# Sums over queries placed directly ahead of the next tile's sums over keys, from the tenth step on

## The chip, the cores and the metric

One Trainium2 chip, one of its cores. The metric is device time in microseconds (us), the median of several runs. Engines are TensorE (PE, its weight loads PEld), VectorE (DVE), ScalarE (ACT), GpSimd (POOL) and SyncE (SP), which only issues transfers here. Each engine runs its own list of instructions in order; semaphores order them against each other. PSUM has eight banks of 128 x 512 floats, and matmuls write there alone.

## The reference, cut to what matters

A macaron block over 4096 tokens of width 256: half a mixture of experts, an attention layer with its own hidden layer, and again half a mixture of experts. The change lies in the attention layer, whose softmax-free form sums over the 16 heads of one token:

```
q, k, v = (xn @ wq + bq), (xn @ wk + bk), (xn @ wv + bv)      # each b n (16 heads) (16 dims)
fq = elu(q) + 1 ; fk = elu(k) + 1
kv    = einsum('bhnd,bhne->bnde', fk, v)                      # sums over keys, per token
qkv   = einsum('bhnd,bnde->bhne', fq, kv)                     # sums over queries, per token
qk    = einsum('bhnd,bnd->bhn', fq, fk.sum(axis=1))
x     = q_x + (qkv / (qk + 1e-6)) @ wo + bo
h     = gelu(ln(x) @ fc_w + fc_b, approximate=False)
out   = x + h @ proj_w + proj_b
```

The mixture of experts routes each token to one of eight experts with a capacity, and passes the others on unchanged.

## The kernel before

The kernel has three phases: the first experts, a middle loop, and the second experts. The middle loop (lines 595, 803, 1044, 1622 and 2085, one for each engine) takes the 32 tiles of 128 tokens through the attention layer in a software pipeline of 43 steps, counted from 0. In step s, tile s-2 gets q, k and v (`qkv`), tile s-4 its sums over keys (`sum_kv`) and tile s-5 its output (`turn_o`, `project`); tile s-6 enters the hidden layer. Every group of four tiles then goes through the hidden layer (`up_mid`, `down_mid`), two of eight hidden slices a step, from step 10 on. From step 14 on finished groups are also routed for the second experts: turned, given logits, chosen (`choose`), counted, dispatched.

All orders are written out by hand. On PE a step before the change goes: turn of zn (tile s-2); `up_mid` (even slice); in every fourth step logits; `sum_kv(s-4)`; `turn_o(s-5)`; `qkv(s-2)`; `down_mid` (odd slice of the step before); `turn_kv(s-4)`; in two of four steps a turned tile; `project(s-5)`; turn of hn (tile s-6); `up_mid` (odd slice); `sum_att(s-4)`; a turned tile or a count; `down_mid` (even slice).

A tile's attention is this chain. `sum_kv` writes bank B_ATT by 32 products of 128 x 32 weights (`keys`, `values`). ACT copies it to `kvt` (`copy_kvt`), PE turns it into bank B_KV, DVE copies it to `kv` (line 1679). `sum_att` multiplies `kv` with `queries`, again 32 products of 128 x 32 weights, into B_ATT. DVE's `attended` transposes that to `att`, adds and inverts the denominator (`den`) and writes `on`. `turn_o` turns `on` into B_KV; ACT copies that as `ots` (high part, line 1063), DVE writes the low part (`low_o`, line 1569), and `project` multiplies both with `o_w` into bank B_V. DVE adds it to z as `xo` (line 1685) and takes statistics of it; POOL makes the root, and DVE hn. In steps 14, 18, 22, ... DVE's `add_rest` (line 1613, four additions) stands behind these statistics. It empties the down banks into `x_`, and the first `down_mid` of the next group, at the end of the same step, waits for it (`s_x2`).

On ACT a step goes: copy of zn's turn, two gelus of the even slice, `copy_kvt`, the copy of o, the exp table, relu, exp and the copy of v (`qkv`), the copy of hn's turn, two gelus of the odd slice. On DVE: low part of zn, z, `low_o`, zn, statistics and routing steps, x1, the features (line 1673), `kv`, `xo` with its statistics, `add_rest`, low part of h, statistics of the next x1, hn, and from step 10 on `attended` last of all. On POOL: the subtraction of hidden parts (line 795) of the even slice, roots and `xr`, the subtraction of the odd slice.

Three variables in PE's loop (`turn_free`, `v_free`, `kv_free`) hold the semaphore after which a shared bank may be written again.

## Time and profile before

| | us |
|---|---|
| runs (three) | 727.66, 728.11, 729.62 |
| median | 728.11 |
| span of the profiled execution | 726.3 |
| PE busy | 670.9 |
| DVE busy | 481.1 |
| ACT busy | 420.1 |
| POOL busy | 326.5 |

The span runs from the first to the last instruction; some 1.8 us of the median lie around it. TensorE's granted clock is 1.00 of its upper level (2.4 GHz) in every stretch of rows 2 below. Busy times overlap, and a busy PE only says that a product was in flight: the places where PE waits are seen by the idle times in front of an instruction, given in brackets with what ended them. Of the loop, steps 10 to 33 take from 232.5 to 528.8 us, steps 34 to 42 the 68 us behind.

### The profile page before, as it was taken

The page shows a single profiled execution, that of the slowest core. Times are in us where ns is not written, and L with a number is a line of the kernel's source. Part 1 is how long each engine was busy: PE and PEld are TensorE (multiplying, and loading weights), DVE is VectorE, ACT ScalarE, POOL GpSimd, SP SyncE. Part 2 cuts the span into 40 slices and gives each one's busy share as a digit, 9 for nine tenths or more (in the row PEclk, how much of TensorE's full clock was granted, in tenths as well). Part 3 has the DMA queues.
Part 4 walks back from the last instruction along what each step waited for, and adds up shares of the span by engine and source line. Part 5 has one row for each costly group of instructions (what it writes and reads, how often), then busy time and mean ns, then how long its engine had stood idle before and what let it go on. Part 6 is the DMA issues. An engine that isn't in the chain of part 4 may idle for free.

```text
span 726.3 us, 17454 instructions
## 1 busy us (share of the span) xinstructions
PE 670.9 (92%) x6214; PEld 567.6 (78%) x6214; DVE 481.1 (66%) x1332; ACT 420.1 (58%) x841; POOL 326.5 (45%) x493
## 2 busy tenths in 40 slices
PE   7689999998777999999999999999999885999994
PEld 5449999975566788888888888888888663999994
DVE  7856757425688766767777768677676565777751
ACT  5755556502334767676767676766754642766660
POOL 5234563122232453545573664745547563353312
PEclk9879999999999999999999999999999998999998
DMA  8479788404656444544555555555433343567720
GB/s 264 149 241 322 229 270 276 139 29 119 98 99 109 91 66 90 95 87 66 101 86 85 117 84 129 68 108 91 86 73 96 116 132 109 167 215 217 219 93 29
DMA packets 287104, 95.56 MB, mean 132 GB/s; under 512 B 213989, under 2 KB 284737, under 8 KB 287019
## 3 DMA queue, kind: packets, MB, share of 16 engines
q1 hardware_dynamic: 272298, 85.48, 48.9%
q0 software_dynamic: 3840, 8.32, 3.6%
q10 hardware_dynamic: 10880, 0.66, 1.0%
q8 instruction: 50, 0.82, 0.5%
q14 instruction: 36, 0.29, 0.1%
HBM read 65.09 MB, written 29.40 MB: 130 GB/s over the span
## 4 chain that ended last, share of the span: by engine, by line
PE 75%; DVE 8%; issue 6%; ACT 4%; POOL 2%; DMA 2%; SPq 1%; ACTq 1%; POOLq 0%; DVEq 0%
PE bank L1735 68%; PE bank L1744 7%; DMA qkv_rows<-feats 1%; POOL hids L795 1%; SPq L373 1%; ACTq L373 1%; ACT hids L1038 1%; DMA x_all<-in_L_attn_q_x_dram 1%; ACT feats L1001 1%; POOL table L677 1%; ACT feats L999 0%; DVE kv_ L1679 0%; ACT ots L1063 0%; DVE sth L1687 0%; DVE att_ L1576 0%
## 5 line engine op out<-in xcount | busy, mean ns | idle before, releaser
L1735 PE MATMUL bank<-down_w,hids 128*128 128x256 f32 x768 | 105.8, 286 | 1.9 <-POOL hids L795 1.6
L1735 PE MATMUL bank<-hnts,up_w 128*128 128x512 f32 x384 | 104.4, 407 | 0.0
L795 POOL TENSOR_TENSOR hids<-hid,hids 128x512 fp32r<-128x512 f32 x64 | 83.1, 1298 | 41.0 <-ACT hids L1038 40.6
L1735 PEld LDWEIGHTS bank<-down_w,hids 128*128 128x128 f32 x768 | 95.7, 188 | 6.2 <-POOL hids L795 3.4
L1735 PE MATMUL bank<-qkv_w,xnts 128*128 128x256 f32 (+1 forms) x384 | 76.4, 346 | 5.7 <-DVE xnts L1589 4.8
L1735 PEld LDWEIGHTS bank<-hnts,up_w 128*128 128x128 f32 x384 | 67.5, 189 | 11.4
L1735 PEld LDWEIGHTS bank<-qkv_w,xnts 128*128 128x128 f32 x384 | 60.6, 189 | 18.2 <-DVE xnts L1589 7.5
L1035 ACT ACTIVATE hid<-bank,cols 128x512 f32<-128x512 f32 x64 | 44.1, 688 | 45.8 <-PE bank L1735 45.5
L786 POOL TENSOR_SCALAR sth<-sth 128x1 f32<-128x1 f32 x32 | 7.2, 226 | 125.3 <-DVE sth L1601 125.3
L1735 PE MATMUL bank<-a_w,xa_h 128*128 128x256 f32 x256 | 60.2, 379 | 0.0
L1735 PE MATMUL bank<-xa_xt,a_w 128*128 128x256 f32 x384 | 55.1, 294 | 1.4 <-DVE xa_xt L1327 1.4
L1735 PE MATMUL bank<-xb_xt,b_w 128*128 128x256 f32 x384 | 52.9, 287 | 1.4 <-DVE xb_xt L1327 1.4
L1735 PEld LDWEIGHTS bank<-xa_xt,a_w 128*128 128x128 f32 x384 | 49.0, 189 | 3.1 <-DVE xa_xt L1327 1.6
L900 ACT ACTIVATE xa_h<-bank,cols 128x256 f32<-128x256 f32 x64 | 26.8, 470 | 40.8 <-PE bank L1735 40.8
L1735 PEld LDWEIGHTS bank<-a_w,xa_h 128*128 128x128 f32 x256 | 46.3, 190 | 5.1
L1735 PEld LDWEIGHTS bank<-xb_xt,b_w 128*128 128x128 f32 x384 | 48.5, 188 | 2.4 <-DVE xb_xt L1327 1.6
L900 ACT ACTIVATE xb_h<-bank,cols 128x256 f32<-128x256 f32 x64 | 26.9, 471 | 35.0 <-PE bank L1735 35.0
L1569 DVE TENSOR_TENSOR ots<-bank,ots 128x256 fp32r<-128x256 f32 x32 | 13.5, 423 | 50.4 <-ACT ots L1063 50.4
L984 ACT CAST xnts<-bank 128x256 fp32r<-128x256 f32 x32 | 12.0, 374 | 59.9 <-PE bank L1744 57.5
L1038 ACT ACTIVATE hids<-bank,cols 128x512 fp32r<-128x512 f32 x64 | 43.6, 681 | 0.0
L1290 DVE TENSOR_TENSOR b_w<-b_raw,b_w 128x512 fp32r<-128x512 f32 x32 | 23.9, 748 | 22.4 <-ACT b_w L876 22.1
L711 POOL DMA_INDIRECT out_dram<-xb_fin,xb_slot x16 | 17.1, 1067 | 48.2 <-DVE xb_fin L1350 46.1
(272 smaller groups left out, 1546.9 us busy)
## 6 DMA issues: line engine op xcount, KB each, us to landing
qkv_rows<-feats SPq DMA_DIRECT2D x32, 384.0 KB, 3.4
a_raw<-in_L_ffn_w_dram SPq DMA_DIRECT2D x32, 256.0 KB, 4.1
a_w<-in_L_ffn_w_dram SPq DMA_DIRECT2D x32, 256.0 KB, 3.7
b_raw<-in_L_ffn_w_dram SPq DMA_DIRECT2D x32, 256.0 KB, 3.2
b_w<-in_L_ffn_w_dram SPq DMA_DIRECT2D x32, 256.0 KB, 3.0
mid_rows<-x_all SPq DMA_DIRECT2D x8, 512.0 KB, 2.9
x<-mid_rows SPq DMA_DIRECT2D x32, 128.0 KB, 2.4
values<-qkv_rows SPq DMA_DIRECT2D x32, 128.0 KB, 2.9
```

Of the source, the lines that this page charges most:

```text
L373: engine.dma_start(keys[i][t * HEADS:(t + 1) * HEADS, :, t * HD:(t + 1) * HD], qkv_rows[1, rows, :].rearrange("(s t) (h d) -> t h s d", t= ...
L677: pool.indirect_dma_start(table, bass.IndirectOffsetOnAxis(ap=dest_b[g % 2][:, i:i + 1], axis=0), entry_b[g % 2][:, i], None, bounds_check ...
L711: pool.indirect_dma_start(ex.target, bass.IndirectOffsetOnAxis(ap=ex.buf.slot[:, c - ex.first * ST], axis=0), ex.buf.fin[c % 4][:], None, ...
L795: pool.tensor_tensor(hids[1][u % 3][:], hid[u % 2][:], f32(hids[0][u % 3][:]), ALU.subtract).then_inc(s_hidl, 1)
L900: act.activation(ex.buf.h[u % 4][:, i], dst[:, i * CAP:(i + 1) * CAP], ACT.Relu, bias=bias).then_inc(ex.sem.relu, 1)
L984: act.copy(xnts[0][n % 2][:], bank[B_TURN][:, 0:D].rearrange("p (k t) -> p k t", k=KD)).then_inc(s_xnh, 1)
L1035: act.activation(hid[u % 2][:], bank[b][:], ACT.Gelu, bias=bias).then_inc(s_hid, 1)
L1038: act.activation(hids[0][u % 3][:], bank[b][:], ACT.Gelu, bias=bias).then_inc(s_hid, 1)
L1290: dve.tensor_tensor(low[cut], ex.raw[cut], f32(high[cut]), ALU.subtract).then_inc(ex.sem.low1, 1)
L1569: dve.tensor_tensor(ots[1][n % 2][:], bank[B_KV][:, 0:D], f32(ots[0][n % 2][:]), ALU.subtract).then_inc(s_ol, 1)
L1735: return pe.matmul(dst, left, right, start=start, stop=stop, skip_group_check=True)
L1744: return pe.matmul(dst, src, ident[:], is_transpose=True, start=start, stop=stop, skip_group_check=True)
```

## The change

From step 10 on (`MERGE_FROM`), tile s-5's sums over queries are issued directly in front of tile s-4's sums over keys, one step later than before and with nothing between the two. Sums over keys now write B_KV, where kv's turn went already, so that B_ATT is free for sums over queries. `on` is turned behind q, k, v instead of in front of them, and into B_ATT. ACT copies o behind the copy of v; DVE makes o's low part behind the features, and `attended` moves from the end of a step to behind zn of the next one. Below step 10 the old order stands. New waits: sums over keys wait for B_KV (`kv_free`), sums over queries for the low part of the tile before (`s_ol`), which reads B_ATT. The number of instructions that compute something is the same.

```diff
--- before.py
+++ after.py
@@ -322,10 +322,19 @@
         MID_STEPS = NT + 11
         ATTENTION_OVER = NT + 4
         UP_FROM = 10
+        MERGE_FROM = UP_FROM
         STAGED = NG - 1
 
         def at(s, k):
             return s - k if 0 <= s - k < NT else None
+
+        def kv_bank(n):
+
+            return B_ATT if n + 4 < MERGE_FROM else B_KV
+
+        def o_turned(n):
+
+            return bank[B_KV if n + 5 < MERGE_FROM else B_ATT][:, 0:D]
 
         def group_at(s, first):
             g, t = divmod(s - first, GROUP)
@@ -1022,7 +1031,13 @@
                 act.wait_ge(s_st1, n + 1)
                 if n >= 1:
                     act.wait_ge(s_kvturn, n)
-                act.copy(kvt[:], bank[B_ATT][:].rearrange("p (i c) -> p i c", i=4)).then_inc(s_kvt, 1)
+                act.copy(kvt[:], bank[kv_bank(n)][:].rearrange("p (i c) -> p i c", i=4)).then_inc(s_kvt, 1)
+
+            def copy_o(n):
+                act.wait_ge(s_ot, n + 1)
+                if n >= 2:
+                    act.wait_ge(s_wo, n - 1)
+                act.copy(ots[0][n % 2][:], o_turned(n)).then_inc(s_o, 1)
 
             def gelus(g, m):
                 b, u = B_QK if g == STAGED and m % 2 else B_UP, g * KM + m
@@ -1055,12 +1070,8 @@
                     logits_out_b(routed(s, 0), bank[B_V])
                 if at(s, 4) is not None and s != 4:
                     copy_kvt(s - 4)
-                if at(s, 5) is not None:
-                    n = s - 5
-                    act.wait_ge(s_ot, n + 1)
-                    if n >= 2:
-                        act.wait_ge(s_wo, n - 1)
-                    act.copy(ots[0][n % 2][:], bank[B_KV][:, 0:D]).then_inc(s_o, 1)
+                if at(s, 5) is not None and s < MERGE_FROM:
+                    copy_o(s - 5)
                 if routed(s, 1) is not None and routed(s, 1) < NG - 2:
                     identify(routed(s, 1))
                 if at(s, 2) is not None:
@@ -1074,6 +1085,8 @@
                 if s == 4:
                     help_keys(1)
                     copy_kvt(0)
+                if at(s, 5) is not None and s >= MERGE_FROM:
+                    copy_o(s - 5)
                 if routed(s, 1) is not None and routed(s, 1) < NG - 2:
                     soften(routed(s, 1))
                 if s == 3:
@@ -1566,7 +1579,7 @@
 
             def low_o(n):
                 dve.wait_ge(s_o, n + 1)
-                dve.tensor_tensor(ots[1][n % 2][:], bank[B_KV][:, 0:D], f32(ots[0][n % 2][:]), ALU.subtract).then_inc(s_ol, 1)
+                dve.tensor_tensor(ots[1][n % 2][:], o_turned(n), f32(ots[0][n % 2][:]), ALU.subtract).then_inc(s_ol, 1)
 
             def attended(n):
 
@@ -1639,7 +1652,7 @@
 
                     dve.scalar_tensor_tensor(out=z[n1 % 5][:], in0=x1[n1 % 8][:], scalar=st[:, 8:9], in1=bo_row[:],
                                              op0=ALU.mult, op1=ALU.add)
-                if n5 is not None:
+                if n5 is not None and s < MERGE_FROM:
                     low_o(n5)
                 if n1 is not None:
                     if n1 >= 1:
@@ -1647,6 +1660,8 @@
                     dve.tensor_scalar(zn[:, 0:D - 1], x1[n1 % 8][:, 0:D - 1], st[:, 6:7], st[:, 9:10], ALU.subtract,
                                       ALU.mult).then_inc(s_zn, 1)
 
+                if n5 is not None and s > MERGE_FROM:
+                    attended(n5)
                 for half in range(2):
                     g = group_at(s, 15 + half)
                     if g is not None:
@@ -1672,6 +1687,8 @@
                     soft = feats[n2 % 2][:, 0:2 * D]
                     dve.scalar_tensor_tensor(out=soft, in0=bank[B_QK][:], scalar=0.0, in1=soft,
                                              op0=ALU.max, op1=ALU.add).then_inc(s_feat, 1)
+                if n5 is not None and s >= MERGE_FROM:
+                    low_o(n5)
                 if n4 is not None:
                     dve.wait_ge(s_kvturn, n4 + 1)
                     if n4 >= 1:
@@ -1691,7 +1708,7 @@
                 if at(s, 6) is not None:
                     low_h(s - 6)
 
-                if s < UP_FROM and n4 is not None:
+                if s < MERGE_FROM and n4 is not None:
                     attended(n4)
                 if at(s, 0) is not None:
                     dve.wait_ge(s_x[s % 8], 16 * (s // 8 + 2))
@@ -1704,8 +1721,6 @@
                         dve.wait_ge(s_hnt, n5)
                     dve.tensor_scalar(hn[:], xo[n5 % 3][:], st[:, 6:7], st[:, 8:9], ALU.subtract,
                                       ALU.mult).then_inc(s_hn, 1)
-                if s >= UP_FROM and n4 is not None:
-                    attended(n4)
                 if 0 <= s - ATTENTION_OVER - 2 < PAIRS:
                     dve.wait_ge(s_st2, NT)
                     low_weights(E, xb, s - ATTENTION_OVER - 2)
@@ -1989,11 +2004,13 @@
             def sum_kv(n):
 
                 pe.wait_ge(s_kvin[n % 2], 16 * 9 * (n // 2 + 1))
-                if n >= 1:
+                if kv_bank(n) == B_KV:
+                    pe.wait_ge(*kv_free)
+                elif n >= 1:
                     pe.wait_ge(s_att, 4 * n - 3)
                 for i in range(4):
                     for j in range(4):
-                        last = mm(bank[B_ATT][32 * j:32 * j + 32, i * P:(i + 1) * P], values[n % 2][:, set_of(i, j)],
+                        last = mm(bank[kv_bank(n)][32 * j:32 * j + 32, i * P:(i + 1) * P], values[n % 2][:, set_of(i, j)],
                                   keys[n % 2][:, set_of(i, j)], True, True)
                 last.then_inc(s_st1, 1)
 
@@ -2006,6 +2023,8 @@
             def sum_att(n):
                 pe.wait_ge(s_kv, n + 1)
                 pe.wait_ge(s_qin[n % 2], 16 * 8 * (n // 2 + 1))
+                if n + 5 > MERGE_FROM:
+                    pe.wait_ge(s_ol, n)
                 for i in range(4):
                     for j in range(4):
                         last = mm(bank[B_ATT][32 * j:32 * j + 32, i * P:(i + 1) * P], kv[:, i, 32 * j:32 * j + 32],
@@ -2015,7 +2034,7 @@
             def turn_o(n):
                 pe.wait_ge(s_att, 4 * (n + 1))
                 for k in range(KD):
-                    last = turn(bank[B_KV][:, k * P:(k + 1) * P], on[n % 2][:, k * P:(k + 1) * P])
+                    last = turn(o_turned(n)[:, k * P:(k + 1) * P], on[n % 2][:, k * P:(k + 1) * P])
                 last.then_inc(s_ot, 1)
 
             def up_mid(g, m):
@@ -2107,15 +2126,19 @@
                 if s == 4:
                     qkv(s - 2, v_free)
                     v_free = (s_val, s - 1)
+                if at(s, 5) is not None and s > MERGE_FROM:
+                    sum_att(s - 5)
                 if at(s, 4) is not None:
                     sum_kv(s - 4)
-                if at(s, 5) is not None:
+                if at(s, 5) is not None and s < MERGE_FROM:
                     pe.wait_ge(*kv_free)
                     turn_o(s - 5)
                     kv_free = (s_ol, s - 4)
                 if at(s, 2) is not None and s != 4:
                     qkv(s - 2, v_free)
                     v_free = (s_val, s - 1)
+                if at(s, 5) is not None and s >= MERGE_FROM:
+                    turn_o(s - 5)
                 if 0 <= g_down < NG:
                     down_mid(g_down, 2 * j_down + 1)
                 if at(s, 4) is not None:
@@ -2148,7 +2171,7 @@
                     pe.wait_ge(*v_free)
                     turn_logits_b(g, bank[B_V])
                     v_free = (s_bpick, 7 * g + 1)
-                if at(s, 4) is not None:
+                if at(s, 4) is not None and s < MERGE_FROM:
                     sum_att(s - 4)
                 for n in turned_at(s, 1):
                     pe.wait_ge(*kv_free)
```

## Rows read from the trace of the kernel before

**Rows 1.** The page, busy time of engines (engine, us, share, instructions).

```profile
PE 670.9 (92%) x6214; PEld 567.6 (78%) x6214; DVE 481.1 (66%) x1332; ACT 420.1 (58%) x841; POOL 326.5 (45%) x493
```

**Rows 2.** Busy time by stretch: us from:to, length, busy of PE, PEld, DVE, ACT, POOL.

```profile
268.59:280.54 11.95, 11.95 (x130) 10.20 (x129) 7.91 (x18) 8.18 (x14) 5.59 (x10) 1.00 0.46 78
...
329.70:342.25 12.55, 12.34 (x135) 10.24 (x134) 9.29 (x27) 8.40 (x16) 5.06 (x9) 1.00 0.44 75
...
392.04:404.40 12.36, 12.36 (x134) 10.59 (x133) 10.71 (x37) 8.81 (x16) 6.39 (x11) 1.00 0.58 120
528.81:538.98 10.17, 9.93 (x122) 8.33 (x121) 7.31 (x21) 6.54 (x11) 4.47 (x6) 1.00 0.45 66
538.98:549.00 10.02, 10.02 (x120) 8.53 (x119) 7.25 (x28) 4.41 (x9) 3.54 (x5) 1.00 0.19 57
549.00:556.77 7.77, 7.58 (x52) 6.58 (x51) 4.43 (x16) 3.72 (x8) 5.66 (x11) 1.00 0.14 37
```

**Rows 3.** Timeline of PE, step 13: start us, us, instruction, count [idle before].

```profile
268.73 1.65 PE L1735 MATMUL bank<-hnts,up_w 128*128 128x512 f32 x6
...
270.31 1.08 PE L1735 MATMUL bank<-keys,values 128*32 128x128 f32 x32
...
275.48 0.96 PE L1735 MATMUL bank<-o_w,ots 128*128 128x256 f32 x6
...
277.99 1.08 PE L1735 MATMUL bank<-queries,kv_ 128*32 128x128 f32 x32
279.00 1.70 PE L1735 MATMUL bank<-down_w,hids 128*128 128x256 f32 x12
```

**Rows 4.** Timeline of PE's weight loads, around a block of sums.

```profile
270.30 0.81 PEld L1735 LDWEIGHTS bank<-keys,values 128*32 128x32 f32 x32 [0.37 <-issue]
...
271.31 0.20 PEld L1744 LDWEIGHTS bank<-ident,on 128*128 128x128 f32 x2 [0.20 <-issue]
```

**Rows 5.** Timeline of PE, logits ahead of sums over keys, step 17.

```profile
318.92 0.64 PE L1735 MATMUL bank<-rb_feat,centred 128*32 128x128 f32 x16
319.38 1.06 PE L1735 MATMUL bank<-keys,values 128*32 128x128 f32 x32
```

**Rows 6.** Timeline of PE, hidden products ahead of a turn, step 36.

```profile
553.66 1.63 PE L1735 MATMUL bank<-hnts,up_w 128*128 128x512 f32 x6
...
555.13 0.38 PE L1744 MATMUL bank<-ident,x_ 128*128 128x128 f32 x2
```

**Rows 7.** Timeline of ACT and DVE, step 13.

```profile
271.57 0.59 ACT L1025 COPY kvt_<-bank 128x512 f32<-128x512 f32 x1
...
272.45 1.28 ACT L1069 ACT_TABLE_LOAD   x1
...
272.46 0.43 DVE L1569 TENSOR_TENSOR ots<-bank,ots 128x256 fp32r<-128x256 f32 x1 [1.85 <-ACT ots L1063]
...
275.13 0.69 DVE L1673 SCALAR_TENSOR_TENSOR feats<-bank,feats 128x512 f32<-128x512 f32 x1 [1.33 <-ACT feats L1001]
```

**Rows 8.** Timeline of DVE and PEld, the four additions and who waits, step 14.

```profile
289.44 1.40 DVE L1613 TENSOR_TENSOR x_<-bank,xr 128x256 f32<-128x256 f32 x4
...
290.95 1.49 PEld L1735 LDWEIGHTS bank<-down_w,hids 128*128 128x128 f32 x12 [0.20 <-DVE x_ L1613]
```

**Rows 9.** Timeline of DVE, first and last operation of `attended`, step 13.

```profile
279.33 0.70 DVE L1576 STREAM_TRANSPOSE att_<-bank 128x512 f32<-128x512 f32 x1
...
280.56 0.43 DVE L1584 TENSOR_TENSOR on<-att_,den 128x256 f32<-128x256 f32 x1
```

**Rows 10.** Denominators: durations min/median/max; one beside POOL; POOL's start in step 13.

```profile
L1578 DVE TENSOR_SCALAR den<-att_ x32: 174/176/982, 187.7 to 549.1; 128x16 f32<-128x16 f32 x32
...
527.90 1.29 POOL L795 TENSOR_TENSOR hids<-hid,hids 128x512 fp32r<-128x512 f32 x1 [0.45 <-ACT hids L1038]
...
528.26 0.96 DVE L1578 TENSOR_SCALAR den<-att_ 128x16 f32<-128x16 f32 x1
...
271.76 1.29 POOL L795 TENSOR_TENSOR hids<-hid,hids 128x512 fp32r<-128x512 f32 x1 [1.42 <-ACT hids L1038]
```

## The prediction

> **What bounds the kernel now.** I read the page first. The matmul engine (PE) is busy 670.9 us, 92% of the span [rows 1]. So a change of order pays only where PE itself gets shorter, and costs wherever PE has to wait. Then I read the busy time by stretch, one stretch to one step of the middle loop [rows 2]. From step 11 to step 33 PE has no idle time to speak of: 11.95 us in a step that only carries the pipeline, 12.36 where turned tiles are added, 12.55 where experts are chosen (0.21 of it idle). Steps 34 to 36 last 10.17, 10.02 and 7.77. Last came the order of PE inside a plain step [rows 3], because the question is which wait ends last at each place in it.
>
> I count from the first hidden product of a step, 268.73 [rows 3]. Sums over keys start at +1.58. Behind them come o's turn, q, k, v, down products and kv's turn; the output projection starts at +6.75, the sums over queries at +9.26, the second down products at +10.27, and the next step at +11.95 [rows 2, 3].
>
> **Part 1: two blocks of 32-column products become one.** Both kinds of sums run as 128x32 products, all others as 128x128. Around such a block the weight loads pause for 0.37 us before it and for 0.20 behind it [rows 4]. Together that is 0.57, the most that a block saves by losing its own entry and exit. It is not all lost time, since the weights otherwise load under running products. From starts: a lone block takes 1.01 (277.99 to 279.00 [rows 3]), but 16 more products of the same kind in front of it only 0.46 [rows 5], so 32 take some 0.88: 0.13 saved. Hidden products in front of a block last 1.58 [rows 3], in front of a 128x128 turn 1.47 (553.66 to 555.13 [rows 6]): 0.11 saved. The first products behind a block start some 0.09 later than elsewhere, an estimate from the spread of those starts. I take 0.33 a merged step, between 0.24 and 0.57. There are 25 merged steps, 11 to 35: 8 us, if nothing else came up.
>
> The Trainium skill says the same in "TensorEngine Tiling (Array Packing)", Key Properties: a change of tiling mode drains the engine. It gives no price, and the sum doesn't rest on it.
>
> **Part 2: what comes late inside a plain step.** In the new order the double block starts at +1.58, its second half at +2.46, and the projection could start 5.17 behind that (270.31 to 275.48 [rows 3]), at +7.63, and the next step at 11.95 - 0.33 = +11.62. Two chains hang on the double block.
>
> Chain A, keys' sums: ScalarE copies them once they end, at 2.46 + 1.08 (a block from first start to last end [rows 3]) + 0.03 = +3.57, where it started at +2.84 before (271.57 [rows 7]). From that copy to VectorE's step on the features is 3.56 (271.57 to 275.13 [rows 7]); o's copy no longer stands between, which gives back 0.29 (271.57 + 0.59 to the table load at 272.45 [rows 7]). So features start at +6.84. The change puts o's low part behind them: +0.65, then 0.43 of its own [rows 7] and 0.11 until PE sees it (as from 290.84 to 290.95 [rows 8]): the projection starts at +8.03, not +7.63. PE waits 0.4 in every step, with nothing else ready in its queue; behind it stand h's turn, hidden and down products. That eats the gain: the step lasts 8.03 + 3.99 = 12.02, so +0.07. Bounds -0.33 (wait covered) and +0.25.
>
> Chain B, queries' sums: VectorE's four steps take 1.66 (279.33 to 280.56 + 0.43 [rows 9]) and start at 1.58 + 1.08 = +2.66. They end at +4.3, in time for o's turn: behind it and ahead of the projection stand twelve down products (some 1.5, as from 279.00 to the next step [rows 3]) and kv's turn, so it is due at about +5.7. But a DVE operation between SBUF tiles stands still while GpSimd works: the denominator took 0.96 beside a GpSimd step of 1.29 and both ended at 529.2, where the median of its group is 176 ns [rows 10]. I call this the lock. Before, it ran with GpSimd idle; now it falls on the subtraction that GpSimd starts 3.0 into the step (271.76 [rows 10]). Then the chain ends at +5.1: still covered here, with 0.6 to spare, but all that stands behind it on VectorE moves 0.8.
>
> The Trainium skill, "SBUF — State Buffer", Who interferes with whom, calls this an exclusive lock of one shared pair of ports. By that rule each of these denominators waits and the sum below is 13; if none did, 7. The trace agrees, in the row just named.
>
> **Part 3: by kinds of step** (us against before; plus is slower).
>
> Step 10 loses its queries' sums (1.1) and gets the later projection (+0.4): -0.7.
>
> Plain steps, eight of them (11 to 13, 17, 21, 25, 29, 33): +0.07 each, +0.6. The logits in some of them only come ahead of the block.
>
> Steps with turned tiles (ten): 15 and 16 have 0.14 more cover before the projection and gain 0.15. In steps 19, 23, 27 and 31 VectorE is busy 10.71 us against 7.91 in the plain step [rows 2]; some 1.9 of these 2.8, statistics and dispatch, now stand behind chain B: 5.1 + 1.9 + 0.4 for the rest's row, then features 0.65, low part 0.43 and 0.11 give a projection at +8.6, so +0.4. In 20, 24, 28 and 32 the same with less, +0.1. Together +1.7; without the lock -1.5.
>
> Steps 14, 18, 22, 26 and 30: here is the dearest part. At the end of the step PE's down products start a new group and need the banks that VectorE empties in four additions (1.40 [rows 8]), which come only behind xo and its statistics, so behind the projection. In step 14 they end at 290.84 and PE loads at 290.95, released by just these [rows 8], exactly when queries' sums ended: that block was the cover. From the projection (+6.75) to these down products (+10.27) are 3.52 [rows 3], and step 14 has the same places. With the block gone PE is done 2.40 behind the projection and still waits the full 3.52: 8.03 + 3.52 + 1.60 = 13.15, so +1.2. Steps 18 to 30 also choose experts; that first step reads q, k, v's bank and now comes behind chain B, so PE's wait there (0.45 in 12.55 [rows 2]) stays. Projection 1.0 later, +1.0 each. Together +5.2; without the lock +4.4. The least is the 0.87 by which the moved block delays the projection, less 0.5: some +2.
>
> Steps 34 to 36 have no q, k, v to put between queries' sums and o's turn, so PE stands before o's turn: it could go at +3.4 (step 36: +2.5) and gets `on` at 2.6 + 1.66 = 4.3, with the lock at 5.1. Step 34: projection at +7.1, then the four additions as above: 12.3 against 10.17. Step 35: low part behind 1.9 of dispatch, projection at +7.5, then 4.05: 11.5 against 10.02. Step 36, which had no queries' sums before: 1.48 + 1.0, wait until 5.1, projection at +7.2, then 4.0: 11.2 against 7.77. That is 2.1 + 1.5 + 3.4 = 7.0; GpSimd's backlog behind step 36 should take up 0.5 of it. Without the lock 4.6 - 0.5.
>
> Queues the moves pass: SyncE's loads of queries wait for queries' sums of a tile two back; these now end at +2.7 of the next step, but the store that SyncE issues first waits for features at +7.5, so nothing is late. Keys' sums now need the bank that turned tiles and counts also use; both are read by +1.4, before +2.46. Weights of the second experts wait for the last queries' sums, which end some 2.6 into step 36 and still far ahead of their use. These cost nothing.
>
> Sum: -0.7 + 0.6 + 1.7 + 5.2 + 6.5 = +13.3, and without the lock -0.7 + 0.6 - 1.5 + 4.4 + 4.1 = +6.9. I take +12, near the upper end, because the row I have shows the lock in full. Span 726.3 + 12 = 738.3; the median of the runs lies 1.8 above the span, so 740.
>
> **Rivals.** (1) Faster: drains are what counts and the late chains are covered, because ScalarE and VectorE are busy only about 8 of 12 us a step [rows 2]. It decides at the projection: if o's low part is ready by +7.63 and the four additions get under way earlier, 25 x 0.33 = 8 is kept against 4 in steps 34 to 36: 724. Against it: the additions already end on the very instant they are needed. Chance 0.08. (2) Nothing to measure: plain steps keep their 0.33, no lock, the last three steps are half absorbed by GpSimd's backlog: 8 x -0.33 - 3.3 + 4.4 + 2 - 0.7 = -0.2, so 728. Chance 0.10. (3) Dearer than forecast: merging saves nothing, because the waits between the two blocks let the engine drain; 25 x 0.3 more: 747. Speaking for it: PE gets three waits there; against it: all are long met. Chance 0.07. (4) The forecast, slower by 7 to 15: 735 to 743, chance 0.75.
>
> What can be told from no change is about 0.3%, 2.2 us. Faster is rival 1 and a fifth of rival 2 that falls below its bound: 0.10. Same is the rest of rival 2 and a hundredth of the forecast: 0.09. Slower is what is left of the forecast, and rival 3: 0.81. The range leaves out rival 1, half of rival 2 and rival 3 beyond a plain overshoot of the sum, no more than 0.2 together: 729 to 745.
>
> **What will show it.** In the trace after: one pause of 0.37 a step instead of two (right for part 1). PE's idle before the projection, released by VectorE's low part, 0.3 to 0.5 in plain steps; if there is none, chain A was mis-sized. In steps 14 to 30 of every fourth, about 1.1 us of PE idle before the down products, released by the additions; if absent, +5.2 goes. PE idle of 1 to 2.5 us before o's turn in steps 34 to 36. Denominators of 0.9 instead of 0.2: the lock. Plain steps under 11.8 us would make the forecast wrong at its root.

## The result, and the profile after

The changed kernel took 745.16 us (median of four runs, 744.44 to 746.28) where the kernel before, on the same chip, took 728.31: a ratio of 1.0226, 95% interval 1.0213 to 1.0239. It is slower by 16.9 us. Its profiled execution has a span of 743.6, 17.3 more than the 726.3 of before. The forecast was 740 with a range to 745, whose end the time just passes, so the side and the main causes were right and the size was some 5 us short. Of the runs below, experiments 10 and 11 had one slow one each (1898 and 1105 us), which their ratios leave out.

The page, busy time of the engines (against rows 1), and the chain that ended last by engine:

```profile
PE 673.9 (91%) x6214; PEld 575.0 (77%) x6214; DVE 509.9 (69%) x1332; ACT 422.8 (57%) x841; POOL 324.4 (44%) x493
...
PE 69%; DVE 17%; issue 6%; ACT 4%; POOL 2%; ACTq 1%; DMA 1%; SPq 0%; POOLq 0%; DVEq 0%
```

PE does no less work than before (673.9 against 670.9), and VectorE is busy 29 us longer with the same 1332 instructions [rows 1]. Now the groups of PE instructions by line, with the idle time in front of them and its releasers:

```profile
L1750 PE MATMUL bank<-down_w,hids 128*128 128x256 f32 x768 | 108.4, 290 | 7.1 <-DVE x_ L1626 5.2 <-POOL hids L804 1.9
...
L1750 PE MATMUL bank<-o_w,ots 128*128 128x256 f32 x192 | 30.5, 294 | 7.9 <-DVE ots L1582 4.0 <-ACT feats L1012 2.7
...
L1759 PE MATMUL bank<-ident,on 128*128 128x128 f32 x64 | 12.8, 282 | 6.6 <-DVE on L1597 6.6
```

These are the three places the prediction named: down products wait for the four additions, the projection waits for o's low part, and o's turn waits for `on` in the last steps. The next view is a step from the inside. The timeline of all engines in step 13, of which rows 3, 4, 7, 9 and 10 show the lines before; the step's first hidden product is at 268.70:

```profile
268.70 1.67 PE L1750 MATMUL bank<-hnts,up_w 128*128 128x512 f32 x6
...
269.79 1.46 POOL L804 TENSOR_TENSOR hids<-hid,hids 128x512 fp32r<-128x512 f32 x1
270.04 1.37 DVE L1660 TENSOR_SCALAR zn_<-x,stz 128x255 f32<-128x255 f32 x1
270.30 0.81 PEld L1750 LDWEIGHTS bank<-queries,kv_ 128*32 128x32 f32 x32 [0.37 <-issue]
270.30 1.08 PE L1750 MATMUL bank<-queries,kv_ 128*32 128x128 f32 x32
...
271.09 0.90 PEld L1750 LDWEIGHTS bank<-keys,values 128*32 128x32 f32 x32
271.20 1.06 PE L1750 MATMUL bank<-keys,values 128*32 128x128 f32 x32
...
271.75 1.29 POOL L804 TENSOR_TENSOR hids<-hid,hids 128x512 fp32r<-128x512 f32 x1 [0.50 <-ACT hids L1053]
...
272.20 0.87 DVE L1591 TENSOR_SCALAR den<-att_ 128x16 f32<-128x16 f32 x1
272.32 0.59 ACT L1034 COPY kvt_<-bank 128x512 f32<-128x512 f32 x1 [0.65 <-PE bank L1750]
...
275.60 0.69 DVE L1688 SCALAR_TENSOR_TENSOR feats<-bank,feats 128x512 f32<-128x512 f32 x1 [1.39 <-ACT feats L1010]
...
276.21 0.41 DVE L1582 TENSOR_TENSOR ots<-bank,ots 128x256 fp32r<-128x256 f32 x1
...
276.77 0.94 PE L1750 MATMUL bank<-o_w,ots 128*128 128x256 f32 x6
```

Read against the prediction: the second half of the double block starts 0.90 behind the first (0.88 forecast), and its weight loads follow without a pause. The copy of keys' sums starts at +3.62 (+3.57), the features at +6.90 (+6.84), the projection at +8.07 (+8.03). The denominator takes 0.87 and ends with GpSimd's subtraction. The tile's durations (ns, min/median/max) say the same for the whole kernel, where rows 10 have a median of 176, and a second instruction has joined it:

```profile
L1591 DVE TENSOR_SCALAR den<-att_ x32: 174/866/1315, 188.1 to 564.8; 128x16 f32<-128x16 f32 x32
...
L1660 DVE TENSOR_SCALAR zn_<-x,stz 128x255 f32<-128x255 f32 x32 | 30.3, 948 | 0.0
```

The second line is of the view by groups. zn took 13.6 us in all before, 424 ns each; now it stands beside GpSimd's subtraction for the odd slice of the step before (269.79, with zn at 270.04 above) and takes 30.3. With the denominators (9.8 us before, 23.3 now) that is VectorE's additional busy time; of the rest, `on` takes 3.8 more and z 3.9 less. The prediction had only the denominators in it. In the plain step zn's part costs nothing, since `attended` starts at +2.75, where +2.66 was forecast.

The plain step was forecast at 12.02 and lasts 12.28. Taken from one step's first hidden product to the next one's, in us:

| steps | before | after | change in all | forecast in all |
|---|---|---|---|---|
| 10 | 12.18 | 11.78 | -0.4 | -0.7 |
| 11, 12, 13 | 11.95 | 12.28, 12.28, 12.36 | } | } |
| 17, 21, 25, 29 | 12.50 | 12.81 | } +2.8 | } +0.6 |
| 33 | 12.36 | 12.81 | } | } |
| 15, 16, 32 | 12.36 | 12.27 | } | } |
| 19, 23, 27, 31 | 12.37 | 12.71 | } +2.3 | } +1.7 |
| 20, 24, 28 | 12.36 | 12.75 | } | } |
| 14 | 11.95 | 13.18 | } | } |
| 18; 22, 26, 30 | 12.56 | 13.27; 13.41 | } +4.5 | } +5.2 |
| 34, 35, 36 | 10.17, 10.03, 7.77 | 12.32, 11.43, 12.46 | +8.2 | +6.5 |

The sum is +17.4, the span's +17.3. Two entries stand out: the plain steps, and step 36 (forecast at 11.2). The first has this cause in the timeline of ACT at the end of step 13, with PE's row at the start of step 13 that shows the same wait one step earlier:

```profile
277.97 0.37 ACT L1000 CAST hnts<-bank 128x256 fp32r<-128x256 f32 x1 [1.86 <-PE bank L1759]
278.36 1.28 ACT L1050 ACT_TABLE_LOAD   x1
279.65 0.69 ACT L1050 ACTIVATE hid<-bank,cols 128x512 f32<-128x512 f32 x1
280.24 0.68 ACT L1053 ACTIVATE hids<-bank,cols 128x512 fp32r<-128x512 f32 x1
...
268.70 1.23 PEld L1750 LDWEIGHTS bank<-hnts,up_w 128*128 128x128 f32 x6 [0.24 <-ACT hids L1053]
```

The even hidden products of the next step need the bank that the second gelu of the odd slice reads last. That gelu stands behind h's turn, the copy of it and a load of the gelu table. It ends 280.92, which is 3.37 us after h's turn starts (277.55) and 2.95 after the copy does; PE starts 281.06. Before, the same chain also took 3.37 from that turn, but the block of sums over queries (1.01) stood between the turn and the next step and covered it. The prediction asked who leaned on that block, found the four additions, and stopped there. There was a second.

Step 36, in PE's timeline and in windows (from:to, length, busy of PE, PEld, DVE, ACT, POOL, granted clock, DMA share, GB/s):

```profile
566.49 0.69 PE L1759 MATMUL bank<-ident,on 128*128 128x128 f32 x2 [2.47 <-DVE on L1597]
566.83 2.91 PE L1750 MATMUL bank<-down_w,hids 128*128 128x256 f32 x12
569.53 0.53 PE L1759 MATMUL bank<-ident,x_ 128*128 128x128 f32 x2
...
563.90:566.49 2.59, 0.12 (x7) 0.01 (x1) 2.30 (x5) 0.41 (x1) 1.93 (x2) 0.98 0.00 0
566.49:570.61 4.12, 4.12 (x22) 4.11 (x23) 1.79 (x7) 0.75 (x2) 1.41 (x2) 0.60 0.39 82
570.61:573.91 3.30, 3.30 (x24) 2.98 (x23) 2.33 (x6) 1.82 (x4) 1.62 (x4) 1.00 0.74 196
```

PE waits 2.47 for `on`, as forecast (o's turn at +5.03; +5.1). Then twelve down products take 2.70 from first start to the next turn instead of some 1.5, because the granted clock is 0.60 over these 4.1 us, most of them at its lower level of 1.2 GHz. Waits of 1.60 in steps 34 and 35 were not followed by that.

### The profile page after: what moved, and what is told of

Same layout as the page of the kernel before. It is cut to its first block, busy times and chain, and to the rows that moved or that the text cites. A ratio compares the mean times of both kernels' runs of the same rounds, so it can differ in the third digit from the quotient of the medians.

```text
span 743.6 us, 17427 instructions
## 1 busy us (share of the span) xinstructions
PE 673.9 (91%) x6214; PEld 575.0 (77%) x6214; DVE 509.9 (69%) x1332; ACT 422.8 (57%) x841; POOL 324.4 (44%) x493
## 4 chain that ended last, share of the span: by engine, by line
PE 69%; DVE 17%; issue 6%; ACT 4%; POOL 2%; ACTq 1%; DMA 1%; SPq 0%; POOLq 0%; DVEq 0%
PE bank L1750 62%; PE bank L1759 7%; DVE den L1591 2%; DVE att_ L1589 2%; DVE x_ L1626 1%; DVE z L1653 1%; POOL hids L804 1%; DVE zn_ L1660 1%; ACT feats L1008 1%; DVE on L1597 1%; ACTq L382 1%; ACT feats L1010 1%; DVE rb_stat L1136 1%; DVE sth L1704 1%; DVE xo L1702 1%
## 5 line engine op out<-in xcount | busy, mean ns | idle before, releaser
L1750 PE MATMUL bank<-down_w,hids 128*128 128x256 f32 x768 | 108.4, 290 | 7.1 <-DVE x_ L1626 5.2
L804 POOL TENSOR_TENSOR hids<-hid,hids 128x512 fp32r<-128x512 f32 x64 | 86.4, 1349 | 28.8 <-ACT hids L1053 28.7
L1303 DVE TENSOR_TENSOR b_w<-b_raw,b_w 128x512 fp32r<-128x512 f32 x32 | 23.9, 748 | 23.3 <-ACT b_w L885 17.0
L1750 PE MATMUL bank<-o_w,ots 128*128 128x256 f32 x192 | 30.5, 294 | 7.9 <-DVE ots L1582 4.0
L1000 ACT CAST hnts<-bank 128x256 fp32r<-128x256 f32 x32 | 11.9, 373 | 44.2 <-PE bank L1759 44.2
```

The costliest lines, as they stand in the source:

```text
L804: pool.tensor_tensor(hids[1][u % 3][:], hid[u % 2][:], f32(hids[0][u % 3][:]), ALU.subtract).then_inc(s_hidl, 1)
L1000: act.copy(hnts[0][g % 2][:, :, t * P:(t + 1) * P], bank[B_TURN][:, 0:D].rearrange("p (k t) -> p k t", k=KD)).then_inc(s_hnh, 1)
L1303: dve.tensor_tensor(low[cut], ex.raw[cut], f32(high[cut]), ALU.subtract).then_inc(ex.sem.low1, 1)
L1750: return pe.matmul(dst, left, right, start=start, stop=stop, skip_group_check=True)
```

## The experiments

The kernel before was run beside each kernel; a difference named below without more is one of spans, from the changed kernel's 743.6. Such a difference also holds what lies outside steps 10 to 40, which comes to as much as 1.3 us (experiment 9), so the argument goes by the lengths of the steps, those of the table above. Each of the first five takes back or mends one cost; the sixth does all five; 7 and 8 add products to the changed kernel; 9, 10 and 12 take from the sixth or add to it, and 11 puts two of the edits into the kernel before.

### 1. The four additions ahead of the projection's residual

```diff
+ if group_at(s, 14) is not None:
+     add_rest(group_at(s, 14))
  if n5 is not None:
      ...                                  # xo and its statistics
- if group_at(s, 14) is not None:
-     add_rest(group_at(s, 14))
```

> The changed kernel (745.2 us) with VectorE's four additions put ahead of xo and its statistics instead of behind them, so that they no longer wait for the output projection. Theory (the moved block was the cover of these additions): the idle of 0.76 to 0.89 us before the group's first down products in steps 14, 18, 22, 26, 30 and 34 goes, 5.2 in all, less 0.5 for xo coming later: 740.5. Rival (another chain of the step, GpSimd's root or ScalarE's gelu, ends as late and takes the wait's place): at most 1 us saved, 744.5, and idle before the same products with another releaser.

Measured: 743.09 us, ratio 1.0189 (1.0172 to 1.0206), span 741.8, only 1.8 less. The wait named by the theory went altogether: steps 14, 18, 22, 26, 30 and 34 are 0.90 to 1.06 shorter, 5.9 in all. But in steps 19, 23, 27 and 31 the projection starts at +9.19 instead of +8.50, 0.70 more a step. (Step 32 is 0.48 longer too, but so it is in experiments 4, 7 and 8: it comes in two lengths, 12.3 and 12.7, whatever the edit.) VectorE and PE's weight loads in step 19:

```profile
351.41 0.68 DVE L1688 SCALAR_TENSOR_TENSOR feats<-bank,feats 128x512 f32<-128x512 f32 x1
352.01 0.41 DVE L1582 TENSOR_TENSOR ots<-bank,ots 128x256 fp32r<-128x256 f32 x1
...
352.54 0.79 PEld L1750 LDWEIGHTS bank<-o_w,ots 128*128 128x128 f32 x6 [1.03 <-issue]
```

VectorE has no idle time in front of the features there: from z on, which itself waits 0.77 for GpSimd's root, it runs from one operation to the next. While PE waited for the additions, VectorE caught up; without that wait it is late one step on, and hn of step 18 starts 0.04 behind the first hidden product of step 19 instead of 0.93 ahead of it. So the idle time in front of the additions measured a wait, not what its removal gives.

### 2. The gelu table fetched early

```diff
+ if 0 <= g_up < NG and at(s, 2) is not None:
+     touch(ACT.Gelu)          # an activation of one column, behind the copy of o
  if at(s, 6) is not None:
      turn_h(s - 6)
```

> The changed kernel with ScalarE's gelu table loaded by a one-column gelu ahead of the copy of h's turn, in the 1.9 us in which ScalarE idles there, up to step 33. Theory (what I missed: the next step's hidden products wait until the second gelu of the odd slice has read their bank, and that gelu is late by the later projection plus the table load): the gap of 0.35 to 0.47 between zn's turn and the hidden products falls to 0.14 in nine steps, 2.1 us: 743.1. Rival (the gap is PE's own, from the order of turns and loads): gap and time stay, 745.2.

Measured: 741.38 us, ratio 1.0174 (1.0157 to 1.0191), span 739.1, 4.5 less. The theory's part came out in place: the plain steps go from 12.28 to 12.02, those with logits from 12.81 to 12.57, and the hidden products no longer wait for ACT. That is the missing term of the forecast, some 0.26 in each of eight steps. More came on top, which no theory had: steps 20, 24 and 28 lose 0.49 each (projection +8.07 instead of +8.53). Timeline of VectorE in step 20:

```profile
358.73 0.17 DVE L1599 TENSOR_SCALAR den<-att_ 128x16 f32<-128x16 f32 x1
...
359.23 1.12 DVE L1605 TENSOR_TENSOR on<-att_,den 128x256 f32<-128x256 f32 x1
```

In the changed kernel the denominator of this step starts together with GpSimd's even subtraction (both at 361.08) and takes 1.31, and `on` behind it 0.42. Here the denominator starts 0.03 ahead of the subtraction (358.76) and takes 0.17, and `on` takes 1.12. So `on` is done at +5.10 instead of +5.55. What moved the start by these few hundredths is not shown. With step 10 (0.23 less) the steps make up 3.9 of the 4.5.

### 3. GpSimd's subtraction behind VectorE's `attended`

```diff
  g_up, j_up = divmod(s - 10, GROUP)
+ if at(s, 5) is not None and s > MERGE_FROM:
+     pool.wait_ge(s_att, 4 * (s - 4))
  if 0 <= g_up < NG:
      low_hidden(g_up, 2 * j_up)
```

> The changed kernel with GpSimd's even subtraction waiting until VectorE's four steps on the sums over queries are done; GpSimd has time for it until the end of the step. Theory (the lock): denominators fall from a median of 0.87 to 0.18 us, o's turn comes 0.7 to 0.8 earlier in steps 34 to 36 (2.2 us, and some 0.5 more from the clock in step 36), the projection 0.24 earlier in seven steps with turned tiles (1.6): 740.9. Rival (a denominator this near to a transpose just takes 0.87, or GpSimd's later subtraction holds up the down products): denominators or PE idle stay, 745 to 747.

Measured: 741.66 us, ratio 1.018 (1.0159 to 1.0201), span 740.1, 3.5 less. The denominator and GpSimd in step 13, and the group of all denominators:

```profile
271.79 0.17 DVE L1593 TENSOR_SCALAR den<-att_ 128x16 f32<-128x16 f32 x1
...
272.79 1.47 POOL L804 TENSOR_TENSOR hids<-hid,hids 128x512 fp32r<-128x512 f32 x1 [1.96 <-DVE on L1599]
...
L1593 DVE TENSOR_SCALAR den<-att_ x32: 174/175/747, 188.1 to 562.8; 128x16 f32<-128x16 f32 x32
```

The same instruction takes 0.17 once GpSimd is kept off it. Where VectorE was the late one, it shows: -0.45 in steps 19, 23, 24, 27 and 31, and o's turn in steps 34 to 36 at +4.4 instead of +5.0. Step 36 is 1.75 shorter, most of it because its wait, now 1.79, was not followed by a fall of the clock. Plain steps don't move, as the forecast had it (0.6 to spare). Steps 18, 22, 26 and 30 are 0.26 longer: there the projection waits 0.5 for o's low part. Steps 20 and 28 keep their length, although the projection comes at +8.07 in step 20 too: PE then waits 0.26 for ACT ahead of h's turn. The lock is real, and taking it from the denominators is worth 3.5 us, some 1.4 of them by the clock; the forecast put 6.4 on it.

### 4. The last three steps in the old order

```diff
+ MERGE_TO = NT + 2
- if at(s, 5) is not None and s >= MERGE_FROM:
+ if at(s, 5) is not None and MERGE_FROM <= s < MERGE_TO:
  ...                                      # and so on each engine
```

> The changed kernel with the old order from step 34 on (step 33 does the sums over queries of tile 29 at its end, as before). Theory (without q, k, v between them, sums over queries and o's turn stand in series): steps 34 to 36 go back from 12.3, 11.4 and 12.5 to 10.2, 10.0 and 7.8, which is 8.2, less 1.1 for one more block in step 33: 738.1. Rival (the end of the loop is set by GpSimd's and the router's backlog, PE only idles earlier instead of later): at most 3 us, 742.

Measured: 739.11 us, ratio 1.0141 (1.0124 to 1.0158), span 737.0, 6.6 less. Windows of steps 34 to 36:

```profile
538.99:549.15 10.16, 9.91 (x121) 8.32 (x120) 7.57 (x24) 6.54 (x11) 4.47 (x6) 1.00 0.43 64
549.15:559.19 10.04, 10.04 (x120) 8.53 (x119) 6.73 (x28) 4.40 (x9) 3.54 (x5) 1.00 0.21 59
559.19:566.96 7.77, 7.47 (x53) 6.63 (x51) 4.35 (x14) 3.72 (x8) 5.75 (x11) 1.00 0.13 39
```

They are the lengths of rows 2 again. Together they are 8.2 shorter, 1.4 of it the clock's. Step 33 grows by 0.83, as it now holds two blocks of sums over queries, and step 32 has its longer length. What steps 34 to 36 cost reaches the end almost in full: GpSimd's backlog, from which I had taken 0.5 back, absorbs nothing.

### 5. o's copy and low part ahead of exp and the features

```diff
  # ACT: behind relu, ahead of exp, instead of behind the copy of v
+ copy_o(s - 5)
  # DVE: ahead of the features, instead of behind them
+ low_o(n5)
```

> The changed kernel with ScalarE's copy of o between relu and exp, and VectorE's low part of o ahead of the features (in steps 10 to 33). Theory (the projection waits because o's two parts stand last in a chain of kv's copy, table load, relu, exp and features): the projection comes 0.37 sooner in plain steps and up to that in the others, and with it the four additions; some 7 us, 738. Rival (the copy of v, now 0.38 later, frees the projection's bank as late): the wait stays with another releaser, 744 to 745.

Measured: 736.8 us, ratio 1.0115 (1.0096 to 1.0134), span 735.4, 8.2 less, the most that one edit gives. ACT, DVE and PE in step 13 (first hidden product at 267.74):

```profile
273.84 0.37 ACT L1042 CAST ots<-bank 128x256 fp32r<-128x256 f32 x1
...
274.25 0.42 DVE L1584 TENSOR_TENSOR ots<-bank,ots 128x256 fp32r<-128x256 f32 x1 [1.01 <-ACT ots L1042]
...
274.78 0.69 DVE L1692 SCALAR_TENSOR_TENSOR feats<-bank,feats 128x512 f32<-128x512 f32 x1
...
275.43 0.96 PE L1752 MATMUL bank<-o_w,ots 128*128 128x256 f32 x6
```

The projection starts at +7.69, where the forecast had put its earliest (+7.63), and steps 19, 23, 27 and 31 drop from 12.71 to 12.14. So chain A cost 0.4 a step because of the order of one operation on ACT and one on VectorE; the sums themselves were not too late.

### 6. All five

> All five edits together: additions first, gelu table early, GpSimd's even subtraction behind, the old order from step 34, o sooner. Theory (the order itself saves the drains, and its cost lies in these chains alone): the single gains are 2.4, 4.1, 3.8, 6.4 and some 7, together with the drains saved 722, faster than before (728.3) by 0.8%. Rival (the waits only change places, as the additions' did in steps 19, 23, 27 and 31): 729 or more, slower than before.

Measured: 724.05 us, ratio 0.9947 (0.9931 to 0.9964), span 722.0: faster than the kernel before by half a per cent. Windows of steps 13, 19 and 20:

```profile
266.02:277.72 11.70, 11.70 (x131) 10.43 (x130) 8.59 (x18) 8.40 (x15) 5.74 (x10) 1.00 0.47 81
...
338.01:350.77 12.76, 12.38 (x136) 10.82 (x134) 11.17 (x35) 8.95 (x17) 6.77 (x13) 1.00 0.52 112
350.77:362.89 12.12, 12.12 (x135) 10.78 (x134) 10.09 (x24) 8.92 (x17) 8.55 (x16) 1.00 0.60 66
```

The plain step is 11.66, against 11.95 before. Only steps 19, 23, 27 and 31 keep a wait of 0.38 before the projection. Step 33 is the other one that is longer than before (13.28 for 12.36), since it holds two blocks of sums over queries. Singly, the five edits give 1.8, 4.5, 3.5, 6.6 and 8.2, which is 24.6; together 21.6. Part of what they mend is the same: the clock's fall in step 36 (1.4) goes in the third and in the fourth alike.

### 7. One full-array product between the two blocks

```diff
  sum_att(s - 5)
+ pe.wait_ge(*kv_free)
+ mm(bank[B_KV][:, 0:P], ones_bf[:], upto[:], True, True)   # overwritten by the sums behind it
```

> The changed kernel with one 128x128 product of 128 columns, whose result nobody reads, between sums over queries and sums over keys in each merged step. It undoes the merging alone and measures the price of an exit and an entry. Theory (0.24 to 0.33 us for a pair of drains): sums over keys start 1.2 to 1.3 instead of 0.90 behind sums over queries, and the step grows by as much, 25 times: 752 to 755. Rival (drains cost nothing that matters, the change never had a gain to lose): 0.96 and 746.

Measured: 748.52 us, ratio 1.0288 (1.0259 to 1.0317), span 747.1, 3.5 more. Weight loads in step 13:

```profile
270.73 0.81 PEld L1750 LDWEIGHTS bank<-queries,kv_ 128*32 128x32 f32 x32 [0.37 <-issue]
271.74 0.10 PEld L1750 LDWEIGHTS bank<-upto,ones_bf 128*128 128x128 bf16 x1 [0.20 <-issue]
271.90 0.81 PEld L1750 LDWEIGHTS bank<-keys,values 128*32 128x32 f32 x32
272.91 0.77 PEld L1750 LDWEIGHTS bank<-qkv_w,xnts 128*128 128x128 f32 x4 [0.20 <-issue]
```

The second block now starts 1.17 behind the first instead of 0.90. The pause of 0.20 behind a block comes back; that of 0.37 ahead of one does not. It stands behind hidden products of 512 columns and not behind one of 128, so it depends on what runs ahead of the block (the added product is also bf16, where the hidden ones are f32; which of the two matters is not shown). Fifteen steps grow by 0.30, 4.5 us in all; steps 19, 20, 23, 24, 27, 28, 31, 34 and 35, where PE waits for VectorE anyway and longer, grow by nothing. Step 32 has its longer length (+0.46), and step 36 is 1.42 shorter, for which see the next experiment: 3.5 in all.

### 8. Idle products in step 36

```diff
  sum_att(s - 5)
+ if s == NT + 4:
+     pe.wait_ge(*kv_free)
+     for _ in range(8):
+         mm(bank[B_KV][:], ones_bf[:], ..., True, True)    # 512 columns each, result unused
```

> The changed kernel with eight 512-column products into a bank that nobody reads, in step 36 alone, while PE otherwise idles 2.47 us for o's turn. Theory (the granted clock fell to 0.60 in the 4.1 us behind that idle stretch because PE had stood still): the twelve down products behind take 1.5 instead of 2.7 us, the clock stays 1.0, the time falls by 1.2: 744. Rival (the weights of the second experts, loading just then, or something else slows these products): they still take 2.7, 745.2.

Measured: 744.31 us, ratio 1.0227 (1.0209 to 1.0244), span 742.5, 1.1 less. The ratio is that of the changed kernel (1.0226), so the medians show no gain; what follows is from the one profiled execution. The granted clock is 1.00 in every window of step 36, down products take 1.53, and the step 11.04 instead of 12.46 (the rest to 1.1 is step 32 in its longer length). But in experiment 7, without any such products and with the same wait of 2.47, the step also lasted 11.04:

```profile
568.70:571.20 2.50, 0.07 (x4) 0.00 (x0) 2.26 (x5) 0.37 (x1) 1.88 (x2) 1.00 0.00 0
571.20:575.00 3.80, 3.76 (x28) 3.57 (x29) 2.63 (x9) 1.12 (x3) 1.45 (x2) 1.00 0.39 81
```

With a wait of about 2.47 the step was long in four profiled executions (the changed kernel and experiments 1, 2 and 5: 12.4 to 12.5) and short in one. So the fall explains the size of step 36 where it happens (1.4 us); that the eight products prevented it is not shown by one execution. The weights that load just then (the experiment's rival) are not the reason by themselves: the DMA share is 0.39 in the stretch with the clock at 0.60 and in this one alike.

### 9. All five but the additions

The diff is that of experiment 1, taken out of experiment 6.

> Compared with the kernel with all five edits (724.05 us, span 722.0): the four additions go back behind the feature and key copies of the same step. Theory (DVE is late in these steps, and the edit only moves its lateness, but to where the five edits together leave little of it): TensorE waits .9 us again for the additions in steps 14, 18, 22, 26, 30 and 34, 5.4 to 6 in all, and the .38 before the projection in steps 19, 23, 27 and 31 goes (-1.5): span +4, about 726. Rival (the edit is worth nothing even here): span within 0.5 of 722. Second rival (it cost, because of the idle in the steps behind): span 720 or less.

Measured: 727.62 us, ratio 0.9984 (0.9974 to 0.9994), span 725.9, 3.9 more than experiment 6. As the theory says, 0.76 to 0.89 of waiting for the additions is back in steps 14, 18, 22, 26 and 30, and steps 19, 23, 27 and 31 are 12.12. A wait of 0.4 for ACT before h's turn is new in steps 20, 24, 28 and 32, which are 0.5 to 0.6 longer. The edit that gave 1.8 alone gives 3.9 in company; by the steps alone it is 2.5 and 5.2.

### 10. All five, with the blocks parted

The added product is that of experiment 7, in steps 11 to 33.

> All five edits, and one 128-column product of the full array between the sums over queries and the sums over keys of steps 11 to 33 (23 products): the merging is undone and all the rest stays. Theory (what the merging saves is a drain of about .27 to .30 a step, and it reaches the end now that nobody is late): +.27 to .30 in the 19 steps where TensorE waits for nobody, nothing in 19, 23, 27 and 31, which have .38 of idle: span 727.1 to 727.7 instead of 722.0. Rival (the gain of the five edits over the kernel before is not the merging's): span within 1 of 722. Second rival (a kernel in which DVE is in time gives the whole 23 x .54 = 12 us that I put on the drains before the change): span 734.

Measured: 729.69 us, ratio 1.0011 (1.0002 to 1.0019), span 727.9, 5.9 more than experiment 6. Windows of steps 13, 19 and 20:

```profile
267.26:279.28 12.02, 12.02 (x133) 10.46 (x131) 8.58 (x18) 8.42 (x15) 5.74 (x10) 1.00 0.46 79
340.86:353.51 12.65, 12.63 (x136) 10.82 (x135) 11.14 (x34) 8.94 (x17) 6.67 (x13) 1.00 0.53 112
353.51:366.27 12.76, 12.60 (x136) 10.82 (x135) 9.93 (x24) 8.94 (x17) 8.65 (x17) 1.00 0.58 74
```

The plain step is 11.98, 0.32 more, and within 0.03 of the step before the change. The 0.32 also holds the added product's own time, some 0.06 (an estimate: eight products of four times the columns take 1.90 in experiment 8), so that 0.26 is left for the merging. Nor does the product restore the old place: it brings back pauses of 0.20 and 0.06, where the merging took away one of 0.20 and one of 0.37. The plain step before the change, with both of those, is 0.29 longer than that of experiment 6. Steps 19, 23, 27 and 31, with their wait of 0.38, don't grow at all, and steps 20, 24, 28 and 32 grow by 0.63, since a wait of 0.31 for ACT comes up there. So the merging is worth 0.26 to 0.32 where nobody is late. It is all of the gain of experiment 6: with the five edits and without the merging there is none. The sum is just above what the theory expected (5.1 to 5.7), though not made up as written. The 0.54 a step of its second rival is not in the prediction, which took 0.33 and had 0.57 as the most.

### 11. The kernel before, with the two edits it can take

The diffs of experiments 1 and 2, put into the kernel before.

> The kernel before, with those two of the five edits that it can take: the Gelu table is fetched early, and the four additions stand ahead of the projection's residual. Theory (there TensorE never waited for the odd Gelu or for these additions, so neither has anything to give): within 1 us of the kernel before, up or down, spans 725.5 to 727.5. Rival (the two edits speed the step up by themselves, and the gain of the five is theirs): 4 us faster than before or more, in the plain steps first, 11.95 to 11.75.

Measured: 728.52 us, ratio 0.9988 (0.9978 to 0.9998), span 727.1. Its plain steps are those of before:

```profile
268.16:280.11 11.95, 11.95 (x132) 10.20 (x130) 7.92 (x19) 8.26 (x15) 5.58 (x10) 1.00 0.46 79
```

Steps 20, 24, 28 and 32 are 0.15 to 0.19 longer and step 34 is 0.42 shorter, which nearly cancels. So the two edits had nothing to give there. The waits they mend are made by the change.

### 12. o's low part one operation earlier still

```diff
+ low_o(n5)
  dve.scalar_tensor_tensor(out=x1[...], ...)      # the input's residual
- low_o(n5)
```

> All five edits, and DVE takes o's second half one operation earlier (ahead of the input's residual of 128x256, .48 us). Theory (in steps 19, 23, 27 and 31 the projection waits .38 for it, and DVE's order alone is why): the four waits go, -1.5 to -1.6, step 36 unchanged: span 720.4. Rival (DVE is full in these steps, so that the wait comes back in the next operation, the features for the logits): span within 0.3 of 722.0.

Measured: 724.75 us, ratio 0.9939 (0.9921 to 0.9958), span 722.2: no better than experiment 6 by its span, and the two ratios can't be told apart. The waits of 0.38 went (step 19: 12.42 instead of 12.75), and others came: 0.11 for the additions in steps 22, 26 and 30, and this one in step 28, in PE's timeline:

```profile
458.19 0.41 PE L1778 MATMUL bank<-ident,hn_ 128*128 128x128 f32 x2 [0.64 <-ACT rb_feat L870]
```

I had expected 720.4, and the rival has it. What is left of waiting in this kernel moves about when one operation is moved.

## Why the prediction was right, and where it was short

**What bounds the kernel: right.** PE busy at 92% with no idle time meant that whatever makes PE wait costs in full, and that was the result.

**Part 1, 0.33 a merged step: right in size.** Experiment 10 measured 0.32, of which some 0.06 is the added product's own, and the plain steps before the change and of experiment 6 differ by 0.29: inside 0.24 to 0.57 and near the value taken from starts. One of its terms was read wrongly: by rows 5 the second half takes twice 0.46, which is 0.92 and not 0.88; it took 0.90. The sum of both pauses (0.57) would have been wrong, although one of each went: 0.57 of pauses in the weight loads cost PE 0.29 here. By experiment 7 the one of 0.37 also depends on what stands in front of the block.

**Part 2, chain A: right.** Projection at +8.07 for +8.03; experiment 5 puts it to +7.69 by moving o's copy and low part alone. **Chain B: right.** It is covered in plain steps and decides o's turn in steps 34 to 36.

**Part 3, plain steps: short by 2.2 us.** This is the step that failed: "the step lasts 8.03 + 3.99 = 12.02". The 3.99 was taken over from before, as if nothing between projection and next step leaned on the block of sums over queries but what was named. The odd gelu did; experiment 2 gives 0.26 a step back. With that edit the 3.99 is there: 12.06 less 8.05 is 4.01 in step 13. In the kernel before its second half ended 1 us ahead of the next step's hidden products, just about the length of the block that was moved away.

**Turned tiles: near** (+2.3 for +1.7), with 20, 24 and 28 as bad as 19 and its like, not 0.1. **Additions: near** (+4.5 for +5.2); steps 18 to 30 were 0.7 to 0.86 longer instead of 1.0. (The 0.45 that the prediction gives for the wait before q, k, v is not in rows 2, which have 12.55 less 12.34, 0.21.) Experiment 1 adds that this term could not be won back by itself.

**Steps 34 to 36: short by 1.7.** The waits were sized right. Missing was the granted clock of 0.60 behind the longest of them (1.4 us), and the 0.5 for GpSimd's backlog was not there.

**The lock: half its size.** With it 13, without it 7, I wrote; keeping GpSimd off the denominators gave 3.5, the clock's share included. The Trainium skill, "SBUF — State Buffer", Who interferes with whom, calls it an exclusive lock of a shared pair of ports. The trace agrees, with a median of 866 ns against 175 for one instruction. How many us that costs follows from the order of the work, not from the rule: in plain steps it costs nothing.

**The rivals.** The first, that drains count and the chains are covered, gave 724 on two conditions: o's low part ready by +7.63 and the additions sooner. Neither holds in the changed kernel. Where they were made to hold, together with the three other edits, the time was 724.05. That the two numbers agree is chance: the rival's sum kept 8 and paid 4 in steps 34 to 36, and in that kernel steps 34 to 36 cost nothing more and steps 19, 23, 27, 31 and 33 cost 2.5. The second (728: plain steps keep their 0.33, no lock) is out, since plain steps grew and the denominators took 0.87. The third, that the waits between the blocks let the engine drain, is out: the second block's weights followed without a pause.

To take 12 out of a sum of 13.3 went the wrong way. The terms I had not seen, the odd gelu and the clock, both added.

## What to carry to other kernels

Before a block of work is moved on an engine that never waits, list everybody whose result is due behind its old place, not only the first one found: for each, the time from its input to its end against the time PE needs for the same stretch without the block. And a merged order has to be paid for on the other engines too: here it was worth some 0.3 us a step, all of it lost until copies, table loads and additions were moved to where they are due. An edit that removes a wait should be judged with the others in place, since alone it may only hand the lateness to the next step.

## What the runs showed of the hardware that was not expected

- Behind a wait of 2.47 us, in which PE did next to nothing (granted clock 0.98 in that stretch), the next 4.1 us had a granted clock of 0.60, and twelve products took 2.70 us instead of 1.53. Waits of 1.60, and one of 1.79 in experiment 3, were not followed by it, nor was the one of 2.47 in experiment 7. The long step came behind four such waits and the short one behind one; the same wait can thus have either outcome.
- One full-width product between two blocks of 32-column products costs 0.30 to 0.32 us a step here, some 0.06 of it (the estimate of experiment 10) its own time. The pause of 0.37 ahead of such a block is not a fixed price: behind a product of 128 columns it was 0.06 (from 271.84, the end of that product's weight load, to 271.90).
- An instruction of 16 columns on VectorE, 175 ns long, takes up to 1315 ns beside a subtraction on GpSimd. Started 0.03 us ahead of the subtraction instead of together with it, it took 0.17 us for 1.31, and the instruction two behind it 1.12 for 0.42 (step 20, experiment 2 against the changed kernel).
